# Order of the four loads per chunk on SyncE's queue in a chunked gated delta rule

## The reference

```python
def step(Sst, inp):
    q_t, k_t, v_t, a_t, b_t = inp
    Sst = Sst * a_t[..., None, None]
    kv = jnp.einsum('bhd,bhde->bhe', k_t, Sst)
    delta = (v_t - kv) * b_t[..., None]
    Sst = Sst + jnp.einsum('bhd,bhe->bhde', k_t, delta)
    o_t = jnp.einsum('bhd,bhde->bhe', q_t, Sst) * scale
    return (Sst, o_t)
S0 = jnp.zeros((b, H, DK, DV), dtype=h.dtype)
_, o = jax.lax.scan(step, S0, (qs, ks_, vs, als, bts))
```

## Time and profile before

| | |
|---|---|
| Median of 3 executions | 5729.75 us (5720.78 to 5732.9) |
| The profiled execution's own time | 5734.83 us |
| Its span | 5733.0 us |
| Mean granted TensorE clock | 0.957 |
| TensorE matmul busy | 5035.2 us (88%) |
| TensorE weight loads busy | 3284.4 us (57%) |
| VectorE busy | 3899.0 us (68%) |
| ScalarE busy | 3136.9 us (55%) |
| GpSimd busy | 2454.4 us (43%) |
| Bytes moved | 460.53 MB, mean 80 GB/s |
| The stage (2405 to 3435 us) | 1030 us, TensorE busy 904.21, DMA share 0.30, 102 GB/s |

### The profile page before, as it was taken

One profiled execution on the slowest core, in us unless ns is written; L12 is line 12 of the kernel. 1 busy time (PEld: TensorE's weight loads), 2 busy tenths in 40 slices (PEclk: granted clock), 3 DMA queues, 4 the chain that ended last, 5 costly groups with the idle time before them and its releaser, 6 DMA issues. The chain is left out here.

```text
span 5733.0 us, 139949 instructions
## 1 busy us (share of the span) xinstructions
PE 5035.2 (88%) x53847; PEld 3284.4 (57%) x53862; DVE 3899.0 (68%) x6898; ACT 3136.9 (55%) x4796; POOL 2454.4 (43%) x2096
## 2 busy tenths in 40 slices
PE   7788888888798899798889989997988999989984
PEld 3455555555577544477777778886632333337774
DVE  5999999999896955544444434443778988845524
ACT  5899999999654845422222223333544666653322
POOL 1788787888565633344444432221630000002214
PEclk9999999999999999899999999998897999999997
DMA  5202020120211133423333322111643222232256
GB/s 169 56 21 48 18 46 21 31 33 16 62 51 54 51 145 146 172 91 103 102 103 102 103 72 89 56 54 36 154 148 66 46 46 46 46 95 77 86 166 189
DMA packets 442677, 460.53 MB, mean 80 GB/s; under 512 B 228546, under 2 KB 377528, under 8 KB 433840
## 3 DMA queue, kind: packets, MB, share of 16 engines
q1 hardware_dynamic: 419504, 400.74, 24.6%
q10 hardware_dynamic: 14336, 25.76, 1.3%
q0 software_dynamic: 8192, 25.17, 1.3%
HBM read 278.15 MB, written 173.39 MB: 79 GB/s over the span
## 5 line engine op out<-in xcount | busy, mean ns | idle before, releaser
L539 POOL TENSOR_SCALAR attn_u<-attn_rel,attn_aux 128x1024 f32<-128x1024 f32 x512 | 1088.2, 2126 | 257.4 <-DVE attn_nm L568 246.6
L694 PE MATMUL attn_tp<-attn_ident,attn_pr 128*128 128x128 f32 x4096 | 569.6, 282 | 221.3 <-ACT attn_pt L630 219.2
L3428 DVE TENSOR_REDUCE attn_mx<-attn_mp 128x1 f32<-128x512 f32 x1024 | 652.8, 685 | 75.3 <-PE attn_mp L3508 72.3
L694 PEld LDWEIGHTS attn_tp<-attn_ident,attn_pr 128*128 128x128 f32 x4096 | 438.7, 141 | 457.8 <-ACT attn_pt L630 320.8
L560 DVE SCALAR_TENSOR_TENSOR attn_u<-attn_rel,attn_aux,attn_u 128x1024 f32<-128x1024 f32 x512 | 677.7, 1324 | 14.0 <-DVE attn_nm L568 7.3
L654 ACT ACTIVATE attn_pr<-attn_pr,attn_nm 128x1024 f32<-128x1024 f32 x512 | 624.3, 1219 | 50.3 <-DVE attn_nm L568 50.3
L3493 ACT ACTIVATE attn_pt<-attn_st 128x1024 f32<-128x1024 f32 x512 | 506.5, 1024 | 263.3 <-PE attn_st L3519 262.8
L568 DVE CUSTOM_DVE_ANT_0 attn_pr<-attn_u,attn_s 128x1024 f32<-128x1024 f32 x512 | 620.1, 1211 | 21.4 <-DVE attn_u L560 10.3
L630 ACT ACTIVATE attn_pt<-attn_tp 128x512 f32<-128x512 f32 x1024 | 587.8, 665 | 5.4 <-PE attn_tp L694 5.3
L3508 PE MATMUL attn_mp<-attn_kt,attn_qt 96*128 96x512 bf16 x1024 | 375.1, 395 | 17.8 <-DMA attn_ident<-in_ident 17.0
L1688 PE MATMUL gin_pw<-gin_w,gin_xt 128*128 128x512 f32 x768 | 345.4, 603 | 3.2 <-ACT gin_qkv L1640 3.2
(11 more groups left out here) (542 smaller groups left out, 10715.5 us busy)
## 6 DMA issues: line engine op xcount, KB each, us to landing
s_qkv<-gin_qkv SPq DMA_DIRECT2D x32, 1536.0 KB
core_qk<-s_qkv SPq DMA_DIRECT2D x32, 1024.0 KB, 5.0
attn_kt<-s_k SPq DMA_DIRECT2D x192, 128.0 KB, 4.5
attn_qt<-s_q SPq DMA_DIRECT2D x378, 64.0 KB, 2.9
moe_rows<-s_hid_s SPq DMA_DIRECT2D x78, 256.0 KB
core_arow<-s_alr SPq DMA_DIRECT2D x32, 512.0 KB, 3.8
core_grow<-s_gar SPq DMA_DIRECT2D x32, 512.0 KB, 3.7
core_vv<-s_qkv SPq DMA_DIRECT2D x32, 512.0 KB, 3.6
```

The lines of the kernel that those rows point to most:

```text
L539: pool.tensor_scalar(u[:, x % 4], rel[:, z % 2, 1], aux[:, s, 4 + NH + h:5 + NH + h], aux[:, s, 4 + 2 * NH + h:5 + 2 * NH + h], ALU.mult, ...
L694: ins = pe.transpose(tp[k][:, n], pr[:, x % BUF, (4 * k + n) * P:(4 * k + n + 1) * P], ident[:])
L3428: dve.reduce_max(mx[w % 2][:].rearrange("p h t a -> p (h t a)")[:, j:j + 1], bank(("row", number))[:], AX.X).then_inc(m["max_done"], 1)
```

## The change

The two `if` parts for `vv` and `grow` now stand ahead of those for `arow` and `qk`. No load, wait, buffer or engine is added or taken away, and the start of the stage, which loads the first chunks, is untouched.

```diff
             def following(i, x):
                 fits = lambda n: not isinstance(i, int) or i + n < TILES
+                if fits(2):
+                    load_v(i + 2, x + 2)
+                    load_gamma(i + 2, x + 2)
                 if fits(3):
                     load_alpha(i + 3)
                 if fits(4):
                     load_qk(i + 4, x + 4)
-                if fits(2):
-                    load_v(i + 2, x + 2)
-                    load_gamma(i + 2, x + 2)
```

## The result

The changed kernel takes 5767.3 us (5754.28 to 5771.24, 5 runs) against 5730.96 us of the kernel before in the same comparison: ratio 1.0071, 95% interval 1.0061 to 1.0082. It is slower by 36 us by the medians. (The ratio is the comparison's own; the quotient of the two medians is 1.0063.) The forecast was 5725 us, range 5703 to 5752.

The account below looks back on a forecast made before the run. The prediction took TensorE, the busiest engine, with waits for late code, to bound the stage. Decay row 0 and code against loads -5 took the profiled 5734.8 us to 5730, forecast as a median of 5725 us, range 5703 to 5752.

Parts of the forecast that it names:

- What bounds the stage: TensorE is busiest, 904 of 1030 us; its waits on issue, 53.4 and 28.5 us, were read as late code.
- Term A: Decay row `arow` behind `grow` lands at 4.9 us, ahead of its scan: 0 us, upper end +40 us.
- 1.26 us per queued load: Added landing time for a load queued behind another, taken from four back-to-back 512 KB loads at the stage's start.
- rival 1: Decay row lands late at its scan, delaying the whole period 27 times: 5765 to 5770 us, chance 0.08.
- Term B: TensorE's code pieces against loads in flight: 28 fewer meet a load, -8, +3 given back: -5 us.
- rival 2: TensorE's code queues behind three loads at the turn between periods: 5745 to 5762 us, chance 0.15.
- 0 us for queries and keys: `qk`, issued later, is needed only two periods after issue and lands within 6.5 us, so costs nothing.
- a wait at the turn may pull the clock down: Remark against a freed middle of the period: a wait between periods may lower TensorE's clock too; no size given.

Follow-up runs that it names:

- experiment 9: Changed kernel with 60 unused transposes of the identity put ahead of TensorE's stage code, shifting it 120 instructions: 5764.97 us, ratio 1.0053 to the kernel before.
- experiment 1: Against the kernel before, only the decay row `arow` moved behind `grow`; queries and keys keep their place: 5749.99 us, ratio 1.0047.
- experiment 3: Changed kernel with two buffers for decay rows, loaded one chunk further ahead: 5773.68 us, ratio 1.0082 to the kernel before.
- experiment 6: Changed kernel with `grow` waiting for the second scores instead of the third, so the row of four goes out earlier: 5726.85 us, ratio 0.9998 to the kernel before.
- experiment 7: No pauses for scores; decay row, queries and keys, values, running products load once buffers are free, in the dense first half: 5799.34 us, ratio 1.0120 to the kernel before.
- shifted kernels: Changed kernel, kernel before and early row of four, each with 60 unused transposes shifting TensorE's code 120 instructions: 5764.97, 5728.21 and 5721.57 us.
- experiment 8: Kernel before with one pause changed, so the running products `grow` go out right behind the values, not at the turn: 5734.23 us, ratio 1.0006.

## Why the prediction was wrong

**What bounds the stage: right.** The waits on issue were read as late code, and the cuts that move with the code in experiment 9 show it.

**Term A, the decay row: the landing mis-sized, its price nil for another reason.** The step that failed is "behind `grow` it lands at 3.6 + 1.3 = 4.9 us". It landed at 6.1 at the median, and queries and keys took 7.9 us from issue, not 6.5. The 1.26 us per queued load, from the start of the stage, did not carry over: `grow` itself took 3.9 us, not 3.6, the row came 2.2 us behind it, and 0.7 of these are the 1024 KB queued behind, as experiment 1's 4.7 us shows. The fit that the prediction set beside the 1.26 (the Trainium skill, "DMA: Bandwidth & Descriptors", section "Anatomy of one DMA") is given there for transfers that GpSimd issues, and these loads are SyncE's; its 1.2 us misses in the same way. The scans did wait, and by rival 1's rule, microsecond for microsecond, the 22.5 us waited would have been most of the loss. But experiment 3 takes the waits away and gains nothing: the wait stood in parallel with the one for code. Rival 1's condition (a landing after more than 5.9 us) was met, and it cost nothing that shows.

**Term B, code against loads: the step that failed.** It counted how many microseconds a load is in flight (7.5 instead of 12.4) and how many pieces of code meet one, a sixth fewer, at 0.3 us each: -8, with +3 given back for the turn. The count treats all places of the period as alike. Experiments 6 and 7 both have the four loads close together (issued within 2.1 and 6.0 us), in another order but with no reader that waits for them, and differ by 72 us. In experiment 6 the row goes out after the second scores, where TensorE needs few instructions per microsecond, and a piece that starts late still arrives nearly in time. In the changed kernel and in experiment 7 it lies on the runs of 64 matmuls of 32 by 32, where TensorE waits for code even without such a row beside it (0.83 and 1.10 us in the earlier trace rows), so that the delay is passed on nearly whole: the packet of the turn above started 3.4 us late and the wait grew from 0.17 to 3.45. So a load in flight beside the code was not worth 0.3 us wherever it lies; it was worth nothing in one place and over 3 us in another. The term stood at -5; measured was +36, the upper end of rival 2 (+32, given a chance of 0.15) and a little more. The prediction's own sign for rival 2, waits on issue up by over 15 us, was just missed (14.5 over all lines, 1.3 over the two of the earlier trace rows), because part of the idle time is put down to `xm` instead.

**Which load:** moving queries and keys alone costs all of it (1.0075), moving the decay row alone 1.0047. They do not add up. The prediction's rival 2 had them together only, and its 0 us for queries and keys counted only their own reader.

**The clock: a part of it, not a clean one.** Of the 34 us in the stage, 9.7 are the same matmuls at a lower granted clock (0.94 for 0.95 over the stage); in experiment 7 it is 23.4 us at 0.91. The direction is that of the prediction's remark that a wait at the turn may pull the clock down as well. But these are single executions: the one of experiment 6 is busy 890.3 us at 0.97, 13.9 less than the one of before, and its median is the same. The 9.7 are within that spread, the 23.4 are not.

**Edges of code and turns between queues.** The Trainium skill ("Runtime: NRT & Kernel Launch", section "Instruction fetch mechanics") has the cost of a piece's edge mostly hidden. The shifted kernels show waits of up to 3.35 us at such edges, so the measurement decides against it for code as dense as this. The Trainium skill ("DMA: Bandwidth & Descriptors", section "Queues, rings and completion order") has DMA engines take turns between queues by packet, and the prediction took from it that a piece of code waits for one packet and not for the row. The trace does not bear that use of it out: the piece at the turn started some 3.4 us late while 187 packets of the row's loads started ahead of it on 16 engines, though it did not wait for the whole row, which was in flight until 2555.9. Whether the rule itself fails is not decided, since what the trace counts as a packet need not be one in the page's sense.

**What stays open.** How long one piece of code is held up by how many queued bytes was not measured by itself; the delays above are single packets. Why 512 KB at the turn beside `grow` costs 24 us in experiment 1 while taking `grow` away gains nothing in experiment 8 is not explained. That TensorE's waits lower the clock is read from neighbouring periods and was not tried alone.

## What to carry to other kernels

When an engine's waits end on "issue" inside a run of like instructions, ask whether its program is a stream that competes with the data loads; the start of the packets of kind "instruction" tells. If so, put the data loads where that engine executes few instructions per microsecond, and not only where their buffers are free. An on-time landing says that a load is early enough for its reader, not that it is harmless to a third party; a pause that seems needless in a queue may be what keeps it out of the way (experiment 7 without them: +70 us). And before pricing a late load, ask what its reader would be waiting for anyway: two waits side by side cost the longer one.

## What the runs showed of the hardware that was not expected

The same loads, moved within the period, cost up to 70 us in a 1031 us stage without a reader that waits for them (experiment 7). Code packets of 16 KB take about a microsecond to move with or without loads beside them, but one started some 3.4 us late behind a row of loads. A load of 512 KB directly behind another and with 1024 KB behind it took 5.4 us to land at the median, against 3.8 alone and 4.7 with nothing behind it. And the fastest version by its ratio, experiment 6 with its code shifted by 120 instructions, is 0.2% faster than the kernel before (0.9970 to 0.9987), where neither the row's place (0.9998) nor the shift (0.9990, interval up to 1.0000) is by itself clear of no change. It is the best of eleven and was not measured again.
